# Graph attention: the probability transposes of three units in four moved from TensorE to VectorE blocks and transfers within SBUF

## The chip, the cores and the metric

The kernel runs on one core of one Trainium2 chip. The time is device microseconds for one execution: 1087.12 us, the median of 3 runs (1085.82 to 1088.69).

## The reference

The reference is a small network over 1024 nodes with 512 features and 16384 edges: a graph attention, a linear-attention mixer and a feed-forward layer, and then, on the normalised state `xn`, a second block. This case concerns the graph part of the second block. It has two layers, each of which is a masked attention with 8 heads of 64 features, a projection, a batch norm and a small feed-forward with another batch norm:

```
for l in range(2):                         # two layers
    q, k, v = x @ Wq[l].T + bq[l], x @ Wk[l].T, x @ Wv[l].T      # 1024 x 512 each, 8 heads of 64
    for h in range(8):
        s = q_h @ k_h.T / 8 + log(edge count)                    # 1024 x 1024; no edge: out
        p = softmax(s, axis=-1)
        o_h = p @ v_h                                            # contracts over the 1024 keys
    x = batchnorm(x + o @ Wo[l].T + bo[l]); x = batchnorm(x + ffn(x))
```

The block sums up the code; the rest of the reference (first block, mixers, the final small networks) is not touched.

## The kernel before, in words

The attention of one layer is cut into 64 units (`UNITS`). Unit n is one head with 128 query rows: units 16p to 16p+15 are the two heads of pair p, interleaved, for the eight blocks of 128 rows (`unit`, line 53). A unit's life is this:

1. TensorE makes the scores of two units together (`both_heads`, lines 2079 to 2095) into two PSUM slots of 128 x 1024. There are four slots, given out in the order of the job list (`job_table`), so a job can begin only when the job four places before it has been evacuated (`begin`).
2. VectorE evacuates the scores, takes the mask in and the row extreme with it (line 1522), into one of four buffers `SMs` (`SMB` = 4). It waits before that until the probabilities of unit n-4 have been read.
3. ScalarE takes the exponential in place, with the row sums as by-product (`exp_unit`, line 965).
4. "turn": TensorE transposes the 128 x 1024 probabilities in eight 128 x 128 pieces (line 2137 to 2141, helper line 1793) into a PSUM slot, since the next product contracts over the keys.
5. VectorE (even units) or ScalarE (odd units) copies the slot to SBUF, to `PTr` (`turned`, lines 490 to 499; the copies have lines 1121 and 745). `PTr` has two buffers, one for each group of four units (g % 2).
6. "agg": for each group of four units TensorE multiplies the transposed probabilities with the values (`aggregate`, lines 2070 to 2077), 32 matmuls.

The order in which these steps stand on every engine is written out by hand in `attention_order` (lines 58 to 81): the turn of unit m = n - 4 (`LAG`) stands just before the scores of unit n; between them stand the projections "q" (8 a layer) and "k" (8 a layer), and the steps "rsum" and "rsum_bc" that bring the row sums to the output. PE, VectorE and ScalarE all walk this one list in order, so an instruction that waits holds up all that is behind it on its engine. The queue of SyncE (SP) carries loads of weights in this phase and nothing else (lines 557 to 563); in the first layer it starts with a move of the state within SBUF (line 556).

Of the kernel before, what the change touches and what calls it, by code (L numbers as in the profile page):

```python
# [23 lines left out]
N = 1024  # L24
D = 512
E = 16384
P = 128
# [28 lines left out]


def attention_order():

    order = [("q", 0), ("q", 1), ("k", 0), ("k", 1)]  # L60
    for n in range(0, UNITS + LAG + 4, 2):
        m = n - LAG
        if 0 <= m < UNITS:
            order += [("turn", m), ("turn", m + 1)]
        if n < UNITS:
            order += [("score", n), ("score", n + 1)]
        if m >= 16 and m % 16 == 2:
            order.append(("rsum_bc", m // 16 - 1))
        if n % 8 == 2 and 8 <= n < UNITS - 8:
            order.append(("q", n // 8 + 1))  # L70
        if n == 4:
            order.append(("k", 2))
        if n % 16 == 6 and n < UNITS - 16:
            order.append(("k", 2 * (n // 16) + 3))
        if n % 16 == 14 and n < UNITS - 32:
            order.append(("k", 2 * (n // 16) + 4))
# [33 lines left out]
def job_table():  # L110
# [93 lines left out]
def build(nc, a, out):  # L204
# [5 lines left out]
    with ctx:  # L210
# [48 lines left out]
        bns = sb("bns", [P, 8])  # L259

        psum = ctx.enter_context(nc.psum_tensor("slots", [P, 4, N], fp32))

# [90 lines left out]
        for l in range(L):  # L353
# [60 lines left out]
        agg_rounded, agg_rest, last_agg_rounded, last_agg_rest = (  # L414
            sem(n) for n in ("agg_rounded", "agg_rest", "last_agg_rounded", "last_agg_rest"))
        neg_dst_made, distances_made, dst_rows_ready = sem("neg_dst_made"), sem("distances_made"), sem("dst_rows_ready")
        wqn_loaded, wkn_loaded, bias_rows_loaded, wcol_made, ucol_made = (
# [71 lines left out]

        def turned(eng, copy_out, l, n):  # L490
# [7 lines left out]
            copy_out(PTr[:, g % 2, n % 2, :, n // 2 % 2 * P:(n // 2 % 2 + 1) * P], f"turn{l}g", n,  # L498
                     lambda s: s.rearrange("p (s n) -> p s n", s=TT))

# [12 lines left out]
        def _(sp):  # L513
# [42 lines left out]
            sp.dma_start(SXR[:].bitcast(fp32), XTR[:].bitcast(fp32)).then_inc(state_moved, 16)  # L556
            load_weight("w120")
            load_weight("go0")
            sp.wait_ge(psum_full, INDEX[("agg0g", UNITS // 4 - 1)] + 1)
            sp.dma_start(gv1_whole, a["gv1"].rearrange("(k p) n -> p k n", p=P)).then_inc(gv1_loaded, 16)  # L560
            for name in ("gq1", "gk1", "w121", "go1"):
                load_weight(name)

# [177 lines left out]
        def _(act):  # L741
# [205 lines left out]
            for l in range(L):  # L947
# [24 lines left out]

                pt_free = (psum_full, INDEX[("mixout1", 3) if l == 0 else ("agg0g", UNITS // 4 - 1)] + 1)
                taken = [0]
                for step, n in attention_order():
# [6 lines left out]
                    elif step == "k":  # L982
                        pair, hs = n // 2, slice(n % 2 * D, (n % 2 + 1) * D)
                        if pair >= 2:
                            act.wait_ge(psum_full, INDEX[(f"score{l}g", 16 * pair - 17)] + 1)
                        elif pair == 1:
                            act.wait_ge(*pt_free)
                        src = full(act, f"k{l}g", n)
                        nc.scalar.activation(KS[pair % 2][:, 0, hs], src[:, 0:D], ACT.Copy).then_inc(k_rounded, 1)
                    elif step == "score" and n >= 1:  # L990
                        exp_until(n - 1)
                        if n == 55:
                            round_weight(6 + 3 * l)
                    elif step == "turn":
                        exp_until(n)
                        if n % 2 == 1:
# [70 lines left out]
        def _(dve):  # L1067
# [421 lines left out]
            for l in range(L):  # L1489
# [8 lines left out]
                for step, n in attention_order():  # L1498
# [15 lines left out]
                    elif step == "score":  # L1514
                        src = full(dve, f"score{l}g", n)
                        if n >= SMB:
# [8 lines left out]
                    elif step == "turn":  # L1525
                        if n % 2 == 0:
                            turned(dve, copy_out, l, n)
                    elif step == "rsum":
                        src = full(dve, f"rsum{l}g", n)
# [8 lines left out]
                    elif step == "rsum_bc":  # L1538
# [6 lines left out]
                    if step == "turn" and n % 16 == 15:  # L1545
                        dve.wait_ge(probs, UNITS * l + n + 1)
# [158 lines left out]
        def _(pe):  # L1705
# [364 lines left out]
            def aggregate(slot, l, g):  # L2070

                for s in range(TT):
                    for e in range(2):
                        head = 2 * (g // 4) + e
                        last = mm(slot[e * DH:(e + 1) * DH, 0:2 * P], GV[:, s, head * DH:(head + 1) * DH],
                                  PTr[:, g % 2, e, s, :], s == 0, s == TT - 1)
                return last
# [46 lines left out]
            for l in range(L):  # L2124
                if l:
                    pe.wait_ge(gv1_loaded, 16)
                    token_major(f"gv{l}", gv1_whole, XT, ready=lambda k: state(2 * l, k))
                for step, n in attention_order():
                    slot = begin(f"{step}{l}g", n)
                    if step == "q":  # L2130
# [139 lines left out]
```

## Time and profile before

The profile is of one execution that took 1087.95 us in all; its span, from the first instruction to the last, is 1086.0 us, and 1.95 us lie around it.

| | value |
|---|---|
| median of the runs shown | 1087.12 us |
| the profiled execution, its span | 1087.95 us, 1086.0 us |
| PE busy | 1011.1 us, 93% |
| VectorE busy | 632.7 us, 58% |
| ScalarE busy | 493.8 us, 45% |
| GpSimd busy | 246.3 us, 23% |
| data moved by DMA | 37.43 MB in 18528 packets |

How to read it: PE is TensorE's matmul row, PEld its weight loads, DVE VectorE, ACT ScalarE, POOL GpSimd, SP SyncE; SPq is SyncE's issuing of transfers. "L1522" is line 1522 of the kernel. In the timeline each row has the start and the length in us, the engine, line and operation, what is written and read, the shapes, the count, and in square brackets the idle time before it with what ended it. The attention phases of the two layers stand in the span from about 461 to 679 us and from 769 to 986 us.

### The profile page before, as it was taken

The numbers are of one execution on the slowest core, as the hardware profiler recorded it, in microseconds if no ns is written. First come the engines' busy times: TensorE is split into PE (matmuls) and PEld (weight loads), VectorE is DVE, ScalarE is ACT, GpSimd is POOL, SyncE is SP. The second block draws the span as 40 slices with busy tenths as digits, with TensorE's granted clock in tenths as the row PEclk, the third lists the DMA queues.
The fourth block names the chain that finished last, engine by engine and source line by source line (L and its number), as shares of the span: only waits on it lengthen the run. The fifth ranks groups of instructions, "written<-read, shape, count | busy, mean of one in ns | idle before, by whom it ended". The sixth has DMA issues, their size and how long they took to land.

```text
span 1086.0 us, 15726 instructions
## 1 busy us (share of the span) xinstructions
PE 1011.1 (93%) x5787; PEld 721.4 (66%) x5794; DVE 632.7 (58%) x1087; ACT 493.8 (45%) x766; POOL 246.3 (23%) x137
## 2 busy tenths in 40 slices
PE   6999999999989999999999999989899999999925
PEld 2836556888777868777777776734777777767413
DVE  4785576468693245265656663643556566654495
ACT  1674434555524124065555663122555555651144
POOL 2000000899630513200000073011000000470400
PEclk9999999999999999999999999999999999999977
DMA  9101100002000311400001010210000001100202
GB/s 330 49 0 39 40 9 12 1 1 78 1 1 1 116 39 40 155 1 2 1 1 40 1 40 1 77 39 0 1 2 1 1 1 40 40 1 20 80 1 77
DMA packets 18528, 37.43 MB, mean 34 GB/s; under 512 B 3804, under 2 KB 5020, under 8 KB 17950
## 3 DMA queue, kind: packets, MB, share of 16 engines
q1 hardware_dynamic: 15134, 34.37, 9.2%
q10 hardware_dynamic: 3328, 2.15, 0.6%
q8 instruction: 45, 0.74, 0.3%
q14 instruction: 21, 0.17, 0.1%
HBM read 30.22 MB, written 4.19 MB: 32 GB/s over the span
## 4 chain that ended last, share of the span: by engine, by line
PE 75%; DVE 8%; POOL 7%; issue 6%; ACT 3%; DMA 1%; DVEq 0%; SPq 0%; ACTq 0%; POOLq 0%
PE slots L1726 62%; PE slots L1793 12%; POOL MASK L646 2%; POOL MASK L640 1%; POOL KR L645 1%; DMA W<-in_wkT 1%; POOL X L677 1%; POOL PT L637 1%; DVE XT L1464 1%; DVE PT L1522 1%; ACT X L1050 1%; DVE Q1L L1452 0%; DVE X L1610 0%; DVE XT L1485 0%; POOL WL L657 0%
## 5 line engine op out<-in xcount | busy, mean ns | idle before, releaser
L1121 DVE COPY PT<-slots 128x1024 f32<-128x1024 f32 (+1 forms) x65 | 78.9, 1214 | 71.5 <-PE slots L1793 70.4
L1726 PE MATMUL slots<-PT,XN 128*64 128x256 f32 x1024 | 117.6, 382 | 0.0
L1726 PE MATMUL slots<-KS,QS 64*128 64x512 f32 x768 | 105.6, 406 | 7.5 <-DVE KS L1512 3.1
L701 POOL TENSOR_TENSOR QS<-QF,QS 128x512 fp32r<-128x512 f32 x16 | 20.7, 1291 | 357.0 <-PE slots L1793 327.5
L745 ACT ACTIVATE PT<-slots 128x1024 f32<-128x1024 f32 x68 | 69.7, 1024 | 67.3 <-PE slots L1793 62.4
L1726 PEld LDWEIGHTS slots<-PT,XN 128*64 128x64 f32 x1024 | 70.6, 137 | 42.0 <-issue 8.9
L1522 DVE CUSTOM_DVE_ANT_0 PT<-slots,MASK 128x1024 f32<-128x1024 f32 x64 | 75.8, 1222 | 31.7 <-PE slots L1726 31.7
L1522 DVE CUSTOM_DVE_ANT_0 SM<-slots,MASK 128x1024 f32<-128x1024 f32 x64 | 75.8, 1222 | 29.8 <-PE slots L1726 29.8
L1726 PEld LDWEIGHTS slots<-KS,QS 64*128 64x128 f32 x768 | 69.7, 184 | 28.1 <-issue 6.7
L965 ACT ACTIVATE SM<-SM,nm 128x1024 f32<-128x1024 f32 x64 | 73.2, 1144 | 25.2 <-DVE nm L1522 25.2
L965 ACT ACTIVATE PT<-PT,nm 128x1024 f32<-128x1024 f32 x64 | 73.3, 1146 | 19.4 <-DVE nm L1522 19.4
L1726 PE MATMUL slots<-PT 128*128 128x512 bf16 (+3 forms) x401 | 78.8, 367 | 2.8 <-ACT PT L745 1.2
L1793 PE MATMUL slots<-ident,SM 128*128 128x128 f32 x600 | 73.6, 274 | 2.9 <-ACT SM L965 2.6
L1793 PEld LDWEIGHTS slots<-ident,SM 128*128 128x128 f32 x600 | 67.2, 140 | 11.5 <-DVE nm L1522 4.0
L1793 PE MATMUL slots<-ident,PT 128*128 128x128 f32 x580 | 71.7, 276 | 1.7 <-ACT PT L965 1.4
L1793 PEld LDWEIGHTS slots<-ident,PT 128*128 128x128 f32 x580 | 63.2, 140 | 15.0 <-issue 13.4
L1726 PEld LDWEIGHTS slots<-PT 128*128 128x128 bf16 (+2 forms) x408 | 36.7, 114 | 48.2 <-DVE PT L1283 20.8
L1283 DVE TENSOR_SCALAR PT<-PT 128x1024 bf16<-128x1024 f16 x148 | 64.0, 479 | 0.5 <-PE slots L1726 0.4
L637 POOL TENSOR_SCALAR PT<-PT 128x1024 f32<-128x1024 bf16 x8 | 8.4, 1048 | 186.1 <-ACT PT L861 185.5
L1464 DVE SCALAR_TENSOR_TENSOR XT<-slots,cols,XT 128x1024 f32<-128x1024 f32 x16 | 20.5, 1282 | 36.6 <-PE slots L1726 36.6
L1726 PE MATMUL slots<-SXR,WL 128*128 128x512 f32 x104 | 40.8, 393 | 0.0
L1281 DVE TENSOR_SCALAR PT<-PT 128x128 bf16<-128x128 f16 x61 | 15.2, 249 | 43.6 <-PE slots L1726 43.2
(394 smaller groups left out, 2101.9 us busy)
## 6 DMA issues: line engine op xcount, KB each, us to landing
X<-in_x SPq DMA_DIRECT2D x4, 512.0 KB, 11.5
W<-in_wout SPq DMA_DIRECT2D x2, 1024.0 KB, 6.3
W<-in_gq SPq DMA_DIRECT2D x2, 1024.0 KB, 5.1
W<-in_gk SPq DMA_DIRECT2D x2, 1024.0 KB, 5.2
spill<-X SPq DMA_DIRECT2D x4, 512.0 KB, 2.6
SXR<-XTR SPq DMA_DIRECT2D x1, 2048.0 KB, 8.4
W<-in_w SPq DMA_DIRECT2D x2, 1024.0 KB, 4.9
W<-in_go SPq DMA_DIRECT2D x2, 1024.0 KB, 5.3
```

What stands on the lines that cost most here:

```text
L637: nc.gpsimd.tensor_scalar(negm[:, i % 2, :], adj0[:, i, :], -NEG, NEG, ALU.mult, ALU.add).then_inc(negm_made, 1)
L646: link(nc.gpsimd.tensor_scalar(MASK[:, i, :], MASK[:, i, :], 0.5, NO_EDGE, ALU.is_lt, ALU.mult))
L701: nc.gpsimd.tensor_tensor(QS[:, j % 2, 1, :], QF[:], QS[:, j % 2, 0, :].bitcast(fp32), ALU.subtract).then_inc(q_split, 1)
L745: nc.scalar.activation(dst, src, ACT.Copy).then_inc(act_evacuated, 1)
L965: nc.scalar.activation(SMs[n % SMB], SMs[n % SMB], ACT.Exp, bias=nm[:, n % 8:n % 8 + 1], scale=-1.0, accum_out=ls[:, pair % 2, 2 * t + e:2 ...
L1121: nc.vector.tensor_copy(dst, src).then_inc(dve_evacuated, 1)
L1281: nc.vector.tensor_scalar(dstrow[:, b, :], iota[:, t * P:(t + 1) * P], dst_f[:, bass.ds(g + b, 1)], None, ALU.is_equal)
L1283: nc.vector.tensor_scalar(srcrow[:, b, :], iota, src_f[:, bass.ds(g + b, 1)], None, ALU.is_equal).then_inc(onehot_ready, 1)
L1464: nc.vector.scalar_tensor_tensor(XT[:, c, :], src, col(bias, c), XT[:, c, :], ALU.add, ALU.add).then_inc(dve_evacuated, 1)
L1522: nc.vector.tensor_tensor_reduce(out=SMs[n % SMB], in0=src, in1=MASK[:, unit(n)[2], :], scale=-1.0, scalar=-0.1 * NO_EDGE, op0=ALU.add, op ...
L1726: return nc.tensor.matmul(o_, lhsT, rhs, start=start, stop=stop)
L1793: return nc.tensor.transpose(slot_part, src, ident[0:rows, 0:rows])
```

## The change

What it does:

- A new step "flip" takes the place of "turn" for every unit n below 56 with n % 4 != 0: 42 units a layer, 84 in all. The other 22 units a layer keep their turn. Copies of the turns with n below 56 are all ScalarE's now.
- In a flip VectorE transposes the 32 x 32 blocks of the 128 x 1024 probabilities, SBUF to SBUF, into one of three buffers `FL` of 128 x 1024. The blocks are then in place within themselves, but not on the right partitions.
- SP moves the blocks to `PTr` with 16 transfers a unit, each from 32 partitions to 32 partitions with one contiguous run of 1 KB on each (`move_blocks`). For this `PTr` has another order within a partition (block of 32 queries, then key block, then query). SP waits before a unit's transfers until the flip is done and the `PTr` buffer is free; VectorE waits before a flip until the transfers of three flips before have landed; the aggregation waits until the transfers of its units have landed.
- VectorE's evacuation of scores into an `SMs` buffer waits on the flip of unit n-4, where it waited on the transpose on PE.
- The order list: aggregations stand two units later, and "q", "k" and "rsum_bc" have other places. On SP the loads of `w12` and `go` stand behind the transfers of units 45 and 49; the rounding of `go` on ScalarE goes from unit 55 to 59.
- The program is built with `dynamic_dma_scratch_size=4096`, where it had the default; `FL` needs 12 KB on each partition.

```diff
+FLIPS = [n for n in range(UNITS - 8) if n % 4 != 0]
+FLIP_BUFFERS = 3
+FLIPS_BEFORE = {n: i for i, n in enumerate(FLIPS)}
...
-            order += [("turn", m), ("turn", m + 1)]
+            order += [("flip" if i in FLIPS_BEFORE else "turn", i) for i in (m, m + 1)]
...
-        if m >= 4 and m % 4 == 0:
+        if m >= 6 and m % 4 == 2 and m < UNITS - 4:
+            order.append(("agg", m // 4 - 1))
+        if m in (UNITS - 4, UNITS):
             order.append(("agg", m // 4 - 1))
...
-            engine = {"q": V, "k": V, "score": V, "turn": (V, A)[i % 2], "rsum": V, "rsum_bc": V, "agg": A}[step]
+            engine = {"q": V, "k": V, "score": V, "turn": A if i < UNITS - 8 else (V, A)[i % 2], "rsum": V, "rsum_bc": V, "agg": A}[step]
...
-        PTr = PT[:, 0:8192].rearrange("p (b e s n) -> p b e s n", b=2, e=2, s=TT)
+        PTr = PT[:, 0:8192].rearrange("p (b e u s q) -> p b e u s q", b=2, e=2, u=8, s=TT)
...
+            def move_blocks(l, n):
+                i = len(FLIPS) * l + FLIPS_BEFORE[n]
+                sp.wait_ge(flipped, i + 1)
+                pt_free(sp, l, n)
+                own = FL[:, i % FLIP_BUFFERS, :].rearrange("p (j s q) -> p j s q", s=TT, j=4)
+                for b in range(4):
+                    for j in range(4):
+                        sp.dma_start(PTr[32 * j:32 * j + 32, n // 4 % 2, n % 2, n // 2 % 2 * 4 + b, :, :],
+                                     own[32 * b:32 * b + 32, j, :, :]).then_inc(blocks_moved[i % FLIP_BUFFERS], 16)
...
+                for n in FLIPS:
+                    move_blocks(l, n)
+                    if n == 45:
+                        load_weight(f"w12{l}")
+                    if n == 49:
+                        load_weight(f"go{l}")
...
+                    elif step == "flip":
+                        i = len(FLIPS) * l + FLIPS_BEFORE[n]
+                        dve.wait_ge(probs, UNITS * l + n + 1)
+                        if i >= FLIP_BUFFERS:
+                            dve.wait_ge(blocks_moved[i % FLIP_BUFFERS], 16 * 16 * (i // FLIP_BUFFERS))
+                        nc.vector.transpose(FL[:, i % FLIP_BUFFERS, :].rearrange("p (j s q) -> p s j q", s=TT, j=4),
+                                            SMs[n % SMB].rearrange("p (s j q) -> p s j q", s=TT, j=4)).then_inc(flipped, 1)
...
-                        need(f"turn{l}g", 4 * n + 2, 4 * n + 3)
+                        for i in range(4 * n, 4 * n + 4):
+                            if i in FLIPS_BEFORE:
+                                moved(wait, l, i)
+                            else:
+                                need(f"turn{l}g", i)
```

## Rows read from the trace of the kernel before

**Rows 1.** The page: busy time by engine, and the chain by engine.
```profile
PE 1011.1 (93%) x5787; PEld 721.4 (66%) x5794; DVE 632.7 (58%) x1087; ACT 493.8 (45%) x766; POOL 246.3 (23%) x137
PE 75%; DVE 8%; POOL 7%; issue 6%; ACT 3%; DMA 1%; DVEq 0%; SPq 0%; ACTq 0%; POOLq 0%
```

**Rows 2.** Stretches: length; busy of PE, PEld, DVE, ACT, POOL; clock; DMA share; GB/s.
```profile
468.80:653.10 184.30, 182.11 (x1379) 137.90 (x1376) 114.51 (x168) 109.75 (x168) 29.10 (x14) 1.00 0.04 13
776.90:961.20 184.30, 182.11 (x1379) 138.04 (x1375) 114.55 (x168) 109.77 (x168) 29.02 (x14) 1.00 0.04 13
563.30:576.90 13.60, 13.60 (x103) 10.13 (x101) 8.39 (x14) 8.01 (x13) 1.29 (x1) 1.00 0.00 0
```

**Rows 3.** The chain of waits in order of time: start, us, what (one group of four).
```profile
566.99 1.90 PE slots L1793 x16
568.89 4.56 PE slots L1726 x24
573.45 1.75 PE slots L1793 x16
575.20 1.58 PE slots L1726 x12
576.78 0.21 PE slots L1793
576.99 3.60 PE slots L1726 x32
```

**Rows 4.** Groups of DVE, 563.3 to 576.9 us: count | busy, mean ns | idle before.
```profile
L1522 DVE CUSTOM_DVE_ANT_0 SM<-slots,MASK 128x1024 f32<-128x1024 f32 x3 | 3.6, 1223 | 1.9 <-PE slots L1726 1.9
L1121 DVE COPY PT<-slots 128x1024 f32<-128x1024 f32 x2 | 2.5, 1225 | 2.4 <-PE slots L1793 2.3
```

**Rows 5.** Line 1485, the same size from SBUF to SBUF on DVE: ns min/median/max.
```profile
L1485 DVE TENSOR_SCALAR XT<-XT,bns x10: 804/812/817, 697.1 to 1039.7; 128x1024 f32<-128x1024 f32 x10
```

**Rows 6.** Timeline of SP, transfers issued: start, length (of all xN together).
```profile
356.41 0.37 SPq L528 DMA_DIRECT2D W<-in_q  x1
452.79 0.52 SPq L556 DMA_DIRECT2D SXR<-XTR  x1
986.91 0.82 SPq L517 DMA_DIRECT2D BC<-in_rows  x2
1004.83 0.33 SPq L568 DMA_DIRECT2D X<-spill  x1
1005.84 0.26 SPq L574 DMA_DIRECT2D QZ<-in_nb  x1
1006.14 0.55 SPq L572 DMA_DIRECT2D QZ<-in_nw  x2
1008.84 2.32 SPq L580 DMA_DIRECT2D QZ<-in_nw  x6
1011.20 0.39 SPq L582 DMA_DIRECT2D QZ<-in_nb  x1
```

**Rows 7.** Transfers by line: count, KB each, median us from issue to landing.
```profile
spill<-X SPq DMA_DIRECT2D x4, 512.0 KB, 2.6
SXR<-XTR SPq DMA_DIRECT2D x1, 2048.0 KB, 8.4
```

**Rows 8.** Timeline of DVE and ACT at the first turns of layer 0.
```profile
465.42 1.15 ACT L965 ACTIVATE SM<-SM,nm 128x1024 f32<-128x1024 f32 x1
467.58 1.22 DVE L1121 COPY PT<-slots 128x1024 f32<-128x1024 f32 x1
```

**Rows 9.** Timeline of PE at the last groups of layer 0, and layer 1.
```profile
653.09 3.67 PE L1726 MATMUL slots<-PT,XN 128*64 128x256 f32 x32
656.70 1.97 PE L1793 MATMUL slots<-ident,PT 128*128 128x128 f32 x16
660.17 1.97 PE L1793 MATMUL slots<-ident,SM 128*128 128x128 f32 x16
```

**Rows 10.** Stretches as in rows 2, where PE has little to do.
```profile
1030.00:1040.00 10.00, 7.25 (x34) 4.09 (x32) 8.39 (x21) 2.78 (x4) 0.00 (x0) 1.00 0.00 1
1066.00:1086.00 20.00, 11.82 (x69) 6.68 (x67) 10.02 (x23) 6.57 (x7) 0.00 (x0) 0.84 0.31 105
```

More of the change, by code:

```diff
@@ L63, in attention_order @@
         if 0 <= m < UNITS:
-            order += [("turn", m), ("turn", m + 1)]
+            order += [("flip" if i in FLIPS_BEFORE else "turn", i) for i in (m, m + 1)]
         if n < UNITS:
             order += [("score", n), ("score", n + 1)]
-        if m >= 16 and m % 16 == 2:
+        if m >= 16 and m % 16 == 4 or m == UNITS + 2:
             order.append(("rsum_bc", m // 16 - 1))
-        if n % 8 == 2 and 8 <= n < UNITS - 8:
+        if n % 8 == 4 and 8 <= n < UNITS - 8:
             order.append(("q", n // 8 + 1))
@@ L72, in attention_order @@
             order.append(("k", 2))
[L73 to L76, printed above, removed]
+        if n == 8:
+            order.append(("k", 3))
+        if n % 8 == 0 and 16 <= n < UNITS - 16:
+            order.append(("k", n // 8 + 2))
         if m >= 16 and m % 16 == 0:
             order.append(("rsum", m // 16 - 1))
-        if m >= 4 and m % 4 == 0:
+        if m >= 6 and m % 4 == 2 and m < UNITS - 4:
+            order.append(("agg", m // 4 - 1))
+        if m in (UNITS - 4, UNITS):
             order.append(("agg", m // 4 - 1))
@@ L150, in job_table @@
         for step, i in attention_order():
-            engine = {"q": V, "k": V, "score": V, "turn": (V, A)[i % 2], "rsum": V, "rsum_bc": V, "agg": A}[step]
+            if step == "flip":
+                continue
+            engine = {"q": V, "k": V, "score": V, "turn": A if i < UNITS - 8 else (V, A)[i % 2], "rsum": V, "rsum_bc": V, "agg": A}[step]
             jobs.append(((f"{step}{l}g", i), engine))
@@ L259, in build @@
         bns = sb("bns", [P, 8])
+        FL = sb("FL", [P, FLIP_BUFFERS, N])
         psum = ctx.enter_context(nc.psum_tensor("slots", [P, 4, N], fp32))
@@ L415, in build @@
             sem(n) for n in ("agg_rounded", "agg_rest", "last_agg_rounded", "last_agg_rest"))
+        flipped, blocks_moved = sem("flipped"), [sem(f"blocks_moved{r}") for r in range(FLIP_BUFFERS)]
         neg_dst_made, distances_made, dst_rows_ready = sem("neg_dst_made"), sem("distances_made"), sem("dst_rows_ready")
@@ L488, in row_ready, with pt_free @@
             eng.wait_ge(row_loaded[n % 2], 16 * (n // 2 + 1))
-        def turned(eng, copy_out, l, n):
+        def pt_free(eng, l, n):
             g = n // 4
@@ L497, in turned, with moved @@
                 eng.wait_ge(psum_full, INDEX[("mixout1", 3) if l == 0 else ("gv1", 3)] + 1)
-            copy_out(PTr[:, g % 2, n % 2, :, n // 2 % 2 * P:(n // 2 % 2 + 1) * P], f"turn{l}g", n,
-                     lambda s: s.rearrange("p (s n) -> p s n", s=TT))
+        def moved(wait, l, n):
+            i = len(FLIPS) * l + FLIPS_BEFORE[n]
+            wait(blocks_moved[i % FLIP_BUFFERS], 16 * 16 * (i // FLIP_BUFFERS + 1))
+        def turned(eng, copy_out, l, n):
+            g = n // 4
+            pt_free(eng, l, n)
+            half = n // 2 % 2 * 4
+            copy_out(PTr[:, g % 2, n % 2, half:half + 4, :, :].rearrange("p b s q -> p s b q"), f"turn{l}g", n,
+                     lambda s: s.rearrange("p (s b q) -> p s b q", s=TT, b=4))
         LAST_USE = {
@@ L556, in _ @@
             sp.dma_start(SXR[:].bitcast(fp32), XTR[:].bitcast(fp32)).then_inc(state_moved, 16)
[L557 to L562, printed above, removed]
+            def move_blocks(l, n):
[7 more added lines that the diff above has]
+                                     own[32 * b:32 * b + 32, j, :, :]).then_inc(blocks_moved[i % FLIP_BUFFERS], 16)
+            for l in range(L):
+                if l:
+                    sp.wait_ge(psum_full, INDEX[("agg0g", UNITS // 4 - 1)] + 1)
+                    sp.dma_start(gv1_whole, a["gv1"].rearrange("(k p) n -> p k n", p=P)).then_inc(gv1_loaded, 16)
+                    for name in ("gq1", "gk1"):
+                        load_weight(name)
+                for n in FLIPS:
[4 more added lines that the diff above has]
+                        load_weight(f"go{l}")
             sp.wait_ge(psum_full, INDEX[(f"rsum_bc{L - 1}g", H // 2 - 1)] + 1)
@@ L971, in exp_until @@
                         taken[0] += 1
-                pt_free = (psum_full, INDEX[("mixout1", 3) if l == 0 else ("agg0g", UNITS // 4 - 1)] + 1)
+                second_keys_free = (psum_full, INDEX[("mixout1", 3) if l == 0 else ("agg0g", UNITS // 4 - 1)] + 1)
                 taken = [0]
@@ L986, in _ @@
                         elif pair == 1:
-                            act.wait_ge(*pt_free)
+                            act.wait_ge(*second_keys_free)
                         src = full(act, f"k{l}g", n)
@@ L991, in _ @@
                         exp_until(n - 1)
-                        if n == 55:
+                        if n == 59:
                             round_weight(6 + 3 * l)
@@ L1515, in _ @@
                         src = full(dve, f"score{l}g", n)
-                        if n >= SMB:
+                        if n >= SMB and n - SMB in FLIPS_BEFORE:
+                            dve.wait_ge(flipped, len(FLIPS) * l + FLIPS_BEFORE[n - SMB] + 1)
+                        elif n >= SMB:
                             dve.wait_ge(psum_full, INDEX[(f"turn{l}g", n - SMB)] + 1)
@@ L1544, in _ @@
                             nc.vector.tensor_tensor(AGL[:, n, :], AG[:, n, :], AGR[:, n, :].bitcast(fp32), ALU.subtract).then_inc(last_agg_rest, 1)
-                    if step == "turn" and n % 16 == 15:
+                    if step in ("turn", "flip") and n % 16 == 15:
                         dve.wait_ge(probs, UNITS * l + n + 1)
@@ L2075, in aggregate @@
                         last = mm(slot[e * DH:(e + 1) * DH, 0:2 * P], GV[:, s, head * DH:(head + 1) * DH],
-                                  PTr[:, g % 2, e, s, :], s == 0, s == TT - 1)
+                                  PTr[:, g % 2, e, :, s, :], s == 0, s == TT - 1)
                 return last
@@ L2128, in _ @@
                 for step, n in attention_order():
+                    if step == "flip":
+                        continue
                     slot = begin(f"{step}{l}g", n)
```

7 lines of the change are left out of this document (4 added, 3 removed).

## The prediction

> **What bounds the kernel now.** I read the page first, then stretches of the attention phase, then the chain in order of time, then SP's own timeline. On the page the reader is to see PE busy for 93% of the span and 75% of the chain [rows 1]. In the attention phase it is sharper: from 468.8 to 653.1 us PE is busy for 182.1 of 184.3 us at full clock, DVE for 114.5, ACT for 109.8, and the same in layer 1 [rows 2]. So PE's order of work is the time there. One group of four units takes 13.60 us (the aggregation of one group to that of the next), and on the chain it is made of an aggregation of 3.60, two pairs of transposes of 1.90 and 1.75, and scores and projections between them [rows 3]. DVE and ACT have 5.2 and 5.6 us of slack in those 13.6 [rows 2]. SP has nearly nothing to do there.
>
> **What the change removes.** Four turns cost PE 1.90 + 1.75 = 3.65 us a group on the chain [rows 3], one of them 0.91. Three in four go for the 14 groups below unit 56: 42 x 0.91 = 38.3 us a layer, 76.7 in both. PE's group falls from 13.6 to 10.9 us. Nothing else on PE changes in amount; the new places of "q", "k" and the aggregations move work and cost nothing while PE is not the bound, or a few us at the seams if it is.
>
> **VectorE.** It loses two copies a group (1.22 each) and gains three block transposes of 128 x 1024 in fp32. The trace has no such operation. From both sides: the same size from SBUF to SBUF takes 0.81 us in a scale and shift [rows 5], and 1.22 us from PSUM [rows 4]; twice the latter, 2.4, is my upper end for the strided writing. I take 1.2, the nearest in work per element. DVE's group is 8.39 - 2.44 + 3.66 = 9.6 us, below PE's 10.9 (8.4 and 13.2 at the ends). ScalarE has one copy a group where it had two, so 8.0 falls to 7.0. Neither is the next bound by rows, unless the upper end holds.
>
> **SyncE, the term that decides.** Each flip needs 16 transfers, issued one after the other by one queue: 48 a group, 672 a layer, 1344 in all. The reader is to see in SP's timeline that the issuing itself takes time, whatever the size [rows 6]:
> - One row on one partition, 1.9 KB: 0.26 us, and with its small neighbours a new one every 0.300 us (1005.84 to 1008.84 is ten of them). This is the least that I find.
> - Columns over 40 to 120 partitions, 4 bytes on each, six in a row: 1008.84 to 1011.20, 0.393 us each. These carry next to no data, so it is the issuing that costs.
> - Over 128 partitions: 0.33 alone; two in a row 0.41 each.
> - The one transfer from SBUF to SBUF: 0.52 alone, 0.56 with the 0.04 that lies between two (0.26 against the 0.30 from start to start).
>
> A transfer of the change spans 32 partitions, in a run of 16. I take the 0.393 of the six in a row, nearest in partitions and in being issued without a pause; 0.300 and 0.56 are the ends. So a flip costs SP 16 x 0.393 = 6.29 us and a group 18.9 us, against 10.9 on PE and 13.6 before. SP becomes the bound.
>
> Data is not: 2 MB within SBUF landed in 8.4 us and 512 KB in 2.6 [rows 7], so a unit's 512 KB needs 2 to 3 us of the 6.3. The Trainium skill (DMA: Bandwidth & Descriptors, Issuing engines are not separate DMA queues) says that the time to initiate a transfer "is usually small relative to the DMA itself". For the 512 KB spill the row agrees, 0.33 against 2.6; for these transfers of 32 KB the rows speak against it, since the same 0.3 to 0.5 is paid for a sixteenth of the bytes. By that rule data alone would set the pace and the sum would be that of rival 1.
>
> **How the stall runs.** With three buffers a flip waits until the transfers of three flips before have landed. The next two units' transfers take SP 12.6 us, so DVE has time to fill the free buffer before SP runs dry, and SP stays in work without a gap. DVE, though, stands before each flip; behind it wait the evacuations of scores n+4 and n+5, behind them ScalarE's exponentials, and PE finds no free slot. All of them run at SP's pace. The wait for a free `PTr` buffer isn't late: the aggregation two groups before needs transfers that are three flips older. The weight loads on SP add two issues.
>
> **The sum, by layer.** SP starts when the first flip is done. Its probabilities are ready at 466.6 (465.42 + 1.15) and DVE comes to it at 467.58, so with 1.2 us at 468.8 [rows 8]. It issues 42 x 6.29 = 264.2 us. The last lands some 2.0 us later (2.6 less 0.33 for the spill, and smaller). Then group 13 is aggregated, which before began at 653.09 [rows 9]. What is behind it has got shorter: the turns of 58 and 59 and the scores of 62 and 63 (656.70 to 660.17, 3.5 us) stand before it now and are done meanwhile. The difference is 468.8 + 264.2 + 2.0 - 653.1 - 3.5 = +78.4 us. Layer 1 has the same stretches [rows 2]: +156.8 in both. In general it is 42 x 16 x t - 185.8 for an issue time t, which is nothing at t = 0.276. The profiled execution would go from 1087.95 to 1244.8; the median of the runs shown is 0.8 less: **1244 us**. With 0.300: 1119. With 0.56: 1468.
>
> **Rivals.**
> 1. *The issuing is cheaper than any row* (t below 0.276), since both sides are in SBUF and each row is 1 KB in one piece. Then PE is the bound again at 10.9 us a group and the time is 1087.1 - 76.7 = 1010, with 5 to 15 us back where DVE's 9.6 us come late at the seams: 1010 to 1025; with t between 0.22 and 0.276 it lies between that and 1087. For it: the only transfers in a row with rows of many bytes are loads that compete for memory, and the trace has none of this shape. Against: nineteen small issues in a row and none under 0.25, and the one of this kind is the dearest of those issued alone. It ends on the other side of mine; it decides from 0.276 us down.
> 2. *SBUF to SBUF costs what its one row says*, 0.56: a flip takes 9.0 us, a group 27, and the time is 1468.
> 3. *PE's clock falls too.* In my case PE is busy for 10.9 of 18.9 us, 58%. At 72% busy the granted clock stayed at 1.00, at 59% it was 0.84 [rows 10]. At 1.2 GHz throughout, PE's group would double to 21.8 us and pass SP's 18.9: 28 x (21.8 - 13.6) = +230, some 1317. A part of the time at that level would stay hidden behind SP.
> 4. *The transpose on DVE is slow*, 2.4 us: DVE's group is 13.2, hidden behind SP in my case; without SP's limit it leaves 28 x 0.4 = 11 us of gain, 1076.
>
> **How the numbers follow.** SP bound with t from 0.300 to 0.48: 0.60, by itself 1119 to 1360. SP dearer, or with the clock on top (rivals 2 and 3): 0.17. Rivals 1 and 4, faster: 0.19. Near the balance, within 0.3%: 0.04. A measurement of this kernel can tell about 0.3% from no change. I leave out the lower half of the faster cases and the upper half of the dear ones: 1060 to 1400. Faster 0.19, same 0.04, slower 0.77.
>
> **What would show it.** SP's issues of the new line back to back, 0.3 to 0.5 us from start to start, with hardly a pause between units; a group in about 19 us; DVE's idle time before the flips ended by a DMA; PE busy well under 80% between 469 and the end of the phase, and idle for DVE's evacuations; 1344 more issues and 43000 more packets of 1 KB. The prediction fails if SP idles for the flips (then PE or DVE is the bound and rival 1 holds), if the issues take under 0.276 us, or if the landing takes far over 3 us, in which case the three buffers would be the limit and not the issuing.

## The result, and the profile after

The changed kernel takes **1585.45 us** (median of 4 runs, 1583.95 to 1589.10) where the kernel before takes 1086.47 us: a ratio of 1.459 (95% interval 1.456 to 1.463). The prediction was 1244, with a range of 1060 to 1400. Slower was forecast and is right. The size is missed by 341 us and lies outside the range.

The profile is of the execution of 1589.1 us, whose span is 1587.3 us. First the rows of the page that answer to [rows 1] and [rows 7]: busy time by engine, the chain by engine and by line, and the transfers by line.

```profile
PE 1014.6 (64%) x5122; PEld 696.4 (44%) x5122; DVE 661.7 (42%) x1115; ACT 464.3 (29%) x738; POOL 245.4 (15%) x137
PEclk9999999999996766766765699977677676656996
...
SPq 46%; PE 33%; issue 8%; POOL 5%; DVE 5%; ACT 2%; DMA 2%; DVEq 0%; ACTq 0%; POOLq 0%
...
PT<-FL SPq DMA_DIRECT2D x1344, 32.0 KB, 1.8
```

PE has 665 instructions fewer and is still busy for as long, since its granted clock is at 0.6 to 0.7 of full in the slices of the attention phases. It is no longer the bound: the chain, 75% PE before, is 46% SP's issuing. The kernel has 64500 packets more than before (83047 against 18528); 43008 of them are the blocks' 1 KB rows that the prediction counted, the rest are packets of 4 bytes, 16 a transfer. To see what SP does, look at its timeline within a stretch of the attention phase, and at the new line's own durations (nanoseconds, min/median/max).

```profile
559.68 40.50 SPq L588 DMA_DIRECT2D PT<-FL  x62
```

```profile
L588 SPq DMA_DIRECT2D PT<-FL x1344: 507/591/1843, 470.4 to 1462.4; - x192
...
  DVE FL L1575: 555.6, 78
  PE slots L1775: 450.4, 28
DMA to landing us min/median/max: 1.8/1.8/4.9
```

One row of 62 issues with no pause. Each takes 0.591 us, and the next starts 0.04 us after its end. Two others wait for these transfers: VectorE before 78 of its flips, and PE before every aggregation that uses them (28). SP itself waited for a flip only at the start of the two layers, which its list of waits shows (total, times, longest, in us):

```profile
SPq L588 <- DVE FL L1575: 35.4, 2, 19.9
```

Stretches answer to [rows 2]: 400 us of the attention of layer 0, and one group of four, from one aggregation to the next.

```profile
500.00:900.00 400.00, 173.45 (x1003) 118.88 (x1003) 122.12 (x172) 89.66 (x144) 34.90 (x17) 0.70 0.23 56
564.80:595.40 30.60, 13.59 (x77) 9.22 (x77) 9.67 (x17) 6.78 (x11) 1.27 (x1) 0.72 0.22 52
```

The group takes 30.6 us where it took 13.6 (the others of the layer take 30.4 to 31.9). In it PE works 13.59 us, partly at the lower clock, VectorE 9.67 (the prediction had 9.6), and the DMA engines are busy for 22% of the time. Nothing but SP's instruction stream is full. The rows of PE's timeline that answer to [rows 9] are an aggregation in mid-phase and that of group 13, which closes layer 0's flips; in brackets is the idle time before, and what ended it.

```profile
564.83 6.24 PE L1775 MATMUL slots<-PT,XN 128*64 128x256 f32 x32 [16.16 <-DMA PT<-FL]
```

```profile
906.75 5.95 PE L1775 MATMUL slots<-PT,XN 128*64 128x256 f32 x32 [17.03 <-DMA PT<-FL]
```

Before, the aggregation of group 13 began at 653.09 us and took 3.67; now it begins 253.7 us later. In layer 1 the delay of the same aggregation is 503.1 us, so the second layer adds 249.4.

### The profile page after: what moved, and what is told of

Same layout as the page of the kernel before. It is cut to its first block, busy times and chain, and to the rows that moved or that the text cites. A ratio compares the mean times of both kernels' runs of the same rounds, so it can differ in the third digit from the quotient of the medians.

```text
span 1587.3 us, 15786 instructions
## 1 busy us (share of the span) xinstructions
PE 1014.6 (64%) x5122; PEld 696.4 (44%) x5122; DVE 661.7 (42%) x1115; ACT 464.3 (29%) x738; POOL 245.4 (15%) x137
## 2 busy tenths in 40 slices
DMA packets 83047, 81.57 MB, mean 51 GB/s; under 512 B 25308, under 2 KB 69532, under 8 KB 82462
## 4 chain that ended last, share of the span: by engine, by line
SPq 46%; PE 33%; issue 8%; POOL 5%; DVE 5%; ACT 2%; DMA 2%; DVEq 0%; ACTq 0%; POOLq 0%
SPq L588 46%; PE slots L1775 30%; PE slots L1842 3%; POOL MASK L686 2%; DMA PT<-FL 1%; POOL MASK L680 1%; POOL KR L685 1%; POOL X L717 1%; DMA W<-in_wkT 1%; POOL PT L677 0%; ACT X L1090 0%; DVE Q1L L1492 0%; DVE X L1659 0%; POOL WL L697 0%; DVE SM L1636 0%
## 5 line engine op out<-in xcount | busy, mean ns | idle before, releaser
L1775 PE MATMUL slots<-PT,XN 128*64 128x256 f32 x1024 | 179.8, 527 | 450.4 <-DMA PT<-FL 450.4
L1775 PEld LDWEIGHTS slots<-PT,XN 128*64 128x64 f32 x1024 | 109.4, 194 | 522.0 <-issue 511.0
L1575 DVE STREAM_TRANSPOSE FL<-PT 128x1024 f32<-128x1024 f32 x56 | 69.5, 1243 | 380.4 <-DMA PT<-FL 380.4
L1575 DVE STREAM_TRANSPOSE FL<-SM 128x1024 f32<-128x1024 f32 x28 | 34.9, 1245 | 175.2 <-DMA PT<-FL 175.2
L1842 PE MATMUL slots<-ident,SM 128*128 128x128 f32 x376 | 49.9, 277 | 2.7 <-ACT SM L1005 2.6
L785 ACT ACTIVATE PT<-slots 128x1024 f32<-128x1024 f32 x40 | 40.9, 1023 | 29.7 <-PE slots L1842 24.8
L1842 PEld LDWEIGHTS slots<-ident,SM 128*128 128x128 f32 x376 | 41.0, 140 | 17.2 <-issue 10.8
L785 ACT ACTIVATE AG<-slots 128x256 f32<-128x256 f32 x32 | 12.3, 384 | 118.9 <-PE slots L1775 118.8
L697 POOL TENSOR_TENSOR WL<-W,W2R 128x2048 fp32r<-128x2048 f32 x4 | 18.3, 4570 | 170.5 <-ACT W2R L800 170.5
L1775 PE MATMUL slots<-WL,XTR 128*128 128x512 f32 x96 | 38.2, 398 | 0.0
L677 POOL TENSOR_SCALAR PT<-PT 128x1024 f32<-128x1024 bf16 x8 | 8.4, 1048 | 187.4 <-ACT PT L901 186.8
```

What stands on the lines that cost most here:

```text
L697: nc.gpsimd.tensor_tensor(REST[name][:], split_source(pool, name), ROUNDED[name][:].bitcast(fp32), ALU.subtract).then_inc(w_split, 1)
L785: nc.scalar.activation(dst, src, ACT.Copy).then_inc(act_evacuated, 1)
L1575: nc.vector.transpose(FL[:, i % FLIP_BUFFERS, :].rearrange("p (j s q) -> p s j q", s=TT, j=4), SMs[n % SMB].rearrange("p (s j q) -> p s j ...
L1775: return nc.tensor.matmul(o_, lhsT, rhs, start=start, stop=stop)
L1842: return nc.tensor.transpose(slot_part, src, ident[0:rows, 0:rows])
```

## Experiments

### What one issue costs

The kernel before, with ten issues of each of nine forms and then six one at a time added on SP, in a stretch in which SP is idle and nothing waits for it. Here `issue(to, frm)` is one transfer, `quad` and `other` are different sets of 32 partitions, `at(i)` is the i-th run of 256 columns (1 KB), and `landed()` waits for all transfers so far.

```diff
+            for i in range(10):
+                issue(FL[quad(i), at(i)], MASK[other(i), 0, 0:256])
+            landed()
+            for i in range(10):
+                issue(FL[quad(i), i * 256:i * 256 + 16], MASK[other(i), 0, 0:16])
+            landed()
...
+            for i in range(10):
+                issue(FL[quad(i), at(i)], a["x"][32 * i:32 * i + 32, 0:256])
+            landed()
...
+            for i in range(6):
+                issue(FL[quad(i), at(i)], MASK[other(i), 0, 0:256])
+                landed()
```

> The kernel before, with SP issuing sets of ten small transfers in the stretch of layer 0's attention where its queue is idle; they move nothing that the kernel uses. From start to start, in us, by set: A 32 rows x 1 KB from SBUF to SBUF, B the same with 64 bytes a row, C 128 rows x 1 KB SBUF to SBUF, D 16 rows, E 8 rows, F 2 rows, G 32 rows x 1 KB SBUF to DRAM, H the same DRAM to SBUF, I 128 rows DRAM to SBUF, J as A with a wait for landing after each. Theory 1 (what costs is that both sides lie in SBUF): A 0.63 and B the same, G and H 0.38 to 0.45, J 0.52 for each issue. Theory 2 (a run of transfers over 16 engines costs that much wherever the sides lie, since the generator of descriptors falls behind): A, G and H all near 0.6, J near 0.35. Theory 3 (the bytes hold the queue up): B far under A. If the cost grows with the engines used, E and F are cheaper than A and D (0.3 to 0.45); if with the rows, C is dearer than A. The kernel's time should stay at 1087 under all three.

The kernel's time stayed where it was, 1087.49 us (one run). Rows of line 564 (count, duration in ns min/median/max, first and last start): 32 rows of 1 KB within SBUF, the same with 64 bytes, 128 rows, eight rows, two rows, then SBUF to DRAM, DRAM to SBUF, and last the first form with a wait for the landing after each.

```profile
L564 SPq DMA_DIRECT2D FL<-MASK x10: 556/590/592, 462.2 to 467.9; - x10
...
L564 SPq DMA_DIRECT2D FL<-MASK x10: 507/591/592, 469.7 to 475.3; - x10
...
L564 SPq DMA_DIRECT2D FL<-MASK x10: 511/601/1494, 477.1 to 482.8; - x10
...
L564 SPq DMA_DIRECT2D FL<-MASK x10: 624/625/701, 493.4 to 499.9; - x10
...
L564 SPq DMA_DIRECT2D FL<-MASK x10: 562/563/582, 501.7 to 507.2; - x10
...
L564 SPq DMA_DIRECT2D probe<-MASK x10: 338/421/1137, 508.8 to 512.9; - x10
...
L564 SPq DMA_DIRECT2D FL<-in_x x10: 319/421/422, 515.5 to 519.5; - x10
...
L564 SPq DMA_DIRECT2D FL<-MASK x6: 507/507/553, 528.6 to 537.7; - x6
```

From start to start that is 0.633 us within SBUF ((467.9 - 462.2)/9) and, with 0.04 between two, 0.463 with one side in DRAM. So two things add up against the 0.393 of the prediction. Having both sides in SBUF costs 0.17 us (0.591 against 0.421). Standing in a run costs 0.08 to 0.10 (0.591 against 0.507 alone; 0.421 against 0.32 and 0.34 for the first of a run). Bytes cost nothing that shows: 64 bytes a row take as long as 1 KB. Rows cost little: with 2, 8, 16, 32 and 128 rows the median lies between 0.563 and 0.625, and not in that order. This is theory 1, with 0.463 just above its 0.38 to 0.45.

### One issue a unit

The 16 transfers of a unit become one of the same 512 KB, 128 rows of 4 KB. It leaves the partitions where they are, so the blocks are not brought to their places.

```diff
-                for b in range(4):
-                    for j in range(4):
-                        sp.dma_start(PTr[32 * j:32 * j + 32, n // 4 % 2, n % 2, n // 2 % 2 * 4 + b, :, :],
-                                     own[32 * b:32 * b + 32, j, :, :]).then_inc(blocks_moved[i % FLIP_BUFFERS], 16)
+                sp.dma_start(PTr[:, n // 4 % 2, n % 2, n // 2 % 2 * 4:n // 2 % 2 * 4 + 4, :, :],
+                             own).then_inc(blocks_moved[i % FLIP_BUFFERS], 16)
```

> A flip's 16 transfers of 32 x 1 KB become one of 128 rows x 4 KB, with the same bytes, waits and buffers; the blocks are not permuted, so this part of the computation is left out. Theory 1 (the issuing on SP is the bound, 10.13 us a unit): SP falls to about 0.4 us a unit, PE is the bound again, 1010 to 1025 us. Rival (the latency of flip, transfer and three buffers, or DVE's added work, costs as much as the issuing hid): over 1060.

1025.98 us (1023.12 to 1027.76), ratio 0.943 (0.941 to 0.946). The same bytes, the same flips, the same waits, 559 us less than the changed kernel. So it is not the bytes, the flips or the new order. The rows are 4 KB here and not 1 KB, so the number of packets falls with the number of issues; the next experiment and the one with two queues keep the 1 KB rows and part the two. The stretch from 480 to 620 us shows PE busy for 98% and at full clock, with 42% of the DMA engines' time used:

```profile
480.00:620.00 140.00, 137.22 (x991) 95.69 (x988) 118.52 (x170) 83.65 (x140) 17.07 (x10) 1.00 0.42 162
```

### Eight issues a unit

Eight transfers of 64 rows of 1 KB, so a unit has as many 1 KB rows as in the changed kernel and half the issues. Here too the blocks do not change partitions.

```diff
+                for j in range(4):
+                    for b in range(2):
+                        sp.dma_start(PTr[64 * b:64 * b + 64, n // 4 % 2, n % 2, n // 2 % 2 * 4 + j, :, :],
+                                     own[64 * b:64 * b + 64, j, :, :]).then_inc(blocks_moved[i % FLIP_BUFFERS], 16)
```

> A flip's 16 transfers become 8 of 64 rows x 1 KB, the same bytes; the blocks are not permuted as needed. Theory 1 (time by the number of issues): 5.1 us a unit, 15.2 a group, 2 x (42 x 5.1 - 186) = +56 us, 1140 us. Rival (time by bytes or by packets, which stay the same): 1585, as the changed kernel. Rival (an issue of 64 rows is dearer than one of 32): between 1140 and 1300.

1167.78 us (one run), 28 above what was expected.

```profile
L588 SPq DMA_DIRECT2D PT<-FL x672: 461/597/2077, 468.5 to 1041.0; - x168
```

The median, 0.597, is that of the 32-row form. The mean of a unit is 5.36 us, 0.67 an issue, because some issues take up to 2.08. Those long ones coincide with loads of instructions (below). The packets of 1 KB are as many as before, and 418 us of the 499 are gone with half the issues, so it is the issues that cost. With 42 x 5.36 the prediction's own formula gives 225.1 - 185.8 = +39.3 a layer, 1166.

### One unit in four, within SBUF

```diff
-FLIPS = [n for n in range(UNITS - 8) if n % 4 != 0]
+FLIPS = [n for n in range(UNITS - 8) if n % 4 == 2]
...
-                    if n == 45:
+                    if n == 46:
...
-                    if n == 49:
+                    if n == 50:
```

> Only units with n % 4 == 2 are flipped: 14 a layer, 28 in all, with the 16 transfers each; all else as in the changed kernel. Theory 1: SP needs 10.1 to 10.4 us a group, PE 13.6 - 0.9 = 12.7, so SP is hidden and the gain of 28 x 0.91 = 25 us shows: 1062 us, plus up to 10 where the transfers' latency (10 us of issuing and 2 of landing) comes late for the aggregation. Rival (the flip's latency holds the aggregation up in every group): 1090 to 1150.

1081.84 us (1081.46 to 1083.02), ratio 0.995 (0.994 to 0.997): a small gain, some fifth of the 25 us expected, and outside both the 1062 to 1072 of the theory and the 1090 to 1150 of the rival. SP needs 10.4 us of a group of 12.5 to 13.5, so its rate is hidden, and PE's busy time falls by 20.8 us (1011.1 to 990.3 on the pages). But PE's pauses of over 0.25 us between 440 and 1000 us grew from 16.2 us in sum to 32.7. The rows of PE's waits (whole run), and SP's and the chain's around 943 us, show two of the places:

```profile
PE slots L1775 <- DMA PT<-FL: 7.5, 6, 2.9
```

```profile
931.78 10.96 SPq L588 DMA_DIRECT2D PT<-FL  x16
942.78 0.58 SPq L551 DMA_DIRECT2D W<-in_go  x1
```

```profile
942.78 5.89 DMA W<-in_go
948.67 0.02 issue
948.69 1.06 ACT W2R L800
```

A weight load stands in SP's queue behind a unit's 16 issues, is issued at 942.78, and ends on the chain. PE was done with the weights that it overwrites at 929.1, so it could have gone 13.7 us earlier. I expected SP's cover to be enough once its rate was below PE's; here a queue that is 80% full is also a late queue. The two places account for about half of the 16.5 us that the pauses grew by. The new order of the list was never run by itself, so its share of the rest is not shown.

### Two issuing queues

Six of each unit's 16 transfers are issued by ScalarE, ahead of its later exponentials.

```diff
+                move_part(sp, l, n, lambda b, j: (4 * b + j) % 8 < 5)
...
+                    elif step == "flip":
+                        exp_until(n)
+                        move_part(act, l, n, lambda b, j: (4 * b + j) % 8 >= 5)
```

> The changed kernel with 6 of a flip's 16 transfers issued by ScalarE's queue, the other 10 by SP. Theory 1 (the rate is that of the issuing sequencer): SP needs 10 x 0.633 + 0.1 = 6.4 us a unit and ScalarE 3 x 6 x 0.633 + 7 = 18.4 us a group, so a group falls from 31 to about 19.5 us and the time to 1260 to 1330. Rival (both queues share one generator of descriptors, or the transfers themselves are the limit): no change, 1585, and ScalarE's issues are longer than 0.6 us.

1278.6 us (one run), inside the 1260 to 1330 of the theory, and 307 less than with one queue.

```profile
L525 SPq DMA_DIRECT2D PT<-FL x840: 507/592/1989, 467.3 to 1152.1; - x168
L525 ACTq DMA_DIRECT2D PT<-FL x504: 513/614/1973, 467.3 to 1139.4; - x168
```

Both queues issue at their own 0.59 to 0.61 us at the same time: each of ScalarE's 504 issues overlaps one of SP's, and SP's take 0.592 us in the median beside one of ScalarE's and 0.591 without. The price belongs to the issuing engine; nothing that both share is full. The Trainium skill (DMA: Bandwidth & Descriptors, Issuing engines are not separate DMA queues) holds the time to initiate a transfer to be "usually small relative to the DMA itself". For these transfers of 32 KB the trace disagrees: one takes 0.591 us to issue and lands 1.8 us after the issue's start, a third of the time, and the transfers overlap while the issues do not.

### By way of DRAM, three units in four

A unit's block buffer is stored in DRAM in one transfer, and comes back in four, one for each target set of 32 partitions (32 x 4 runs of 1 KB). Five issues with one side in DRAM take the place of 16 within SBUF. The loads of a unit stand behind the store of the next flipped unit.

```diff
+                sp.dma_start(a["bounce"][i % ROUND], FL[:, i % FLIP_BUFFERS, :]).then_inc(put_out[i % FLIP_BUFFERS], 16)
...
+                sp.wait_ge(put_out[i % FLIP_BUFFERS], 16 * (i // FLIP_BUFFERS + 1))
...
+                blocks = a["bounce"][i % ROUND].rearrange("(b q) (j m) -> j q b m", b=4, j=4)
+                for j in range(4):
+                    to = PTr[32 * j:32 * j + 32, n // 4 % 2, n % 2, half:half + 4, :, :].rearrange("p b s q -> p b (s q)")
+                    sp.dma_start(to, blocks[j]).then_inc(blocks_moved[i % ROUND], 16)
...
+                for at, n in enumerate(FLIPS):
+                    put(l, n)
+                    if at:
+                        get(l, FLIPS[at - 1])
```

> A flip's blocks go to DRAM in one transfer of 128 rows x 4 KB and come back in 4 transfers of 32 rows x 4 runs of 1 KB, the next unit's store ahead of this unit's loads; five issues where there were 16. Theory 1 (number of issues times the price of one with a side in DRAM, 0.46): 2.5 us of SP a unit, 7.5 a group, under PE's 10.9; the time is near that of the one-issue kernel, 1026 to 1045. Rival (bytes: 1 MB a unit through 16 engines; 8 x 0.16 + 32 x 0.06 to 0.09 us an engine, 9.6 to 12.5 us a group): transfers become the bound or come late, 1050 to 1100.

1085.62 us (10 runs, 1080.47 to 1091.54), ratio 1.000 (0.998 to 1.002). The 500 us are gone, but so is the gain: my 1026 to 1045 is missed and the rival with the bytes is right in its number (whether also in its cause is the last experiment's question). The rows are the stretch from 480 to 640 us, and over the whole run PE's waits for the loads, SP's waits for the store and the transfers by line:

```profile
480.00:640.00 160.00, 134.03 (x931) 95.64 (x929) 115.02 (x164) 82.26 (x135) 16.97 (x10) 0.96 0.87 262
```

```profile
PE slots L1788 <- DMA PT<-bounce: 47.1, 21, 4.1
```

```profile
SPq L593 <- DMA bounce<-FL: 34.8, 40, 4.4
```

```profile
bounce<-FL SPq DMA_DIRECT2D x84, 512.0 KB, 4.2
PT<-bounce SPq DMA_DIRECT2D x336, 128.0 KB, 3.7
```

### By way of DRAM, two units in four

```diff
-FLIPS = [n for n in range(UNITS - 8) if n % 4 != 0]
+FLIPS = [n for n in range(UNITS - 8) if n % 4 in (1, 3)]
```

> As the kernel through DRAM, but with two units in four flipped (n % 4 of 1 and 3). Theory 1: 56 turns less, 51 us, less the 10 to 16 us of gaps on PE that the one-issue and the one-in-four kernel show: 1046 to 1055. If the rival of the kernel with three in four holds there, this one, with 6.4 to 8.3 us of transfers in a group of 11.8, should be the faster of the two.

**1048.3 us** (1042.46 to 1051.40), ratio 0.966 (0.964 to 0.968). It lies within the 1046 to 1055 expected, leaves nothing of the reference out and is the fastest such version. The diff is against the version with three units in four by DRAM. The same rows as above: PE busy for 98% at full clock, the DMA engines for 60%, and 5.8 us of waits where there were 47.1.

```profile
480.00:640.00 160.00, 156.08 (x1173) 113.81 (x1171) 108.39 (x161) 103.58 (x160) 31.33 (x15) 1.00 0.60 182
```

```profile
PE slots L1788 <- DMA PT<-bounce: 5.8, 4, 1.8
```

```profile
bounce<-FL SPq DMA_DIRECT2D x56, 512.0 KB, 3.2
PT<-bounce SPq DMA_DIRECT2D x224, 128.0 KB, 3.4
```

### Two units in four, within SBUF

The same choice of units as in the last, with the changed kernel's 16 transfers.

> The changed kernel with two units in four flipped (n % 4 of 1 and 3) and the 16 transfers within SBUF, the control for the kernel through DRAM with the same units. Theory 1 (issuing at 10.36 us a unit, the mean of the changed kernel with its longer issues): 28 units a layer take 290 us, 2 x (290 - 186) = +208, 1295 us. Rival (what made the kernel through DRAM fast is that fewer units are flipped, not the number of issues): near 1048.

1305.31 us (one run). The theory's 1295 is 10 us short, and the rival's 1048 is far off. With 28 units a layer instead of 42 the time above before falls from 499 to 218 us. So of the 537 us between the changed kernel (1585) and the last version (1048), fewer units give back 280 and the way by DRAM, with five issues, 257. Fewer units alone leave the kernel 218 us slower than before; only the way by DRAM turns it into a gain.

```profile
L588 SPq DMA_DIRECT2D PT<-FL x896: 507/591/2201, 468.9 to 1178.2; - x180
```

### By way of DRAM, five units in eight

```diff
-FLIPS = [n for n in range(UNITS - 8) if n % 4 != 0]
+FLIPS = [n for n in range(UNITS - 8) if n % 8 in (1, 2, 3, 5, 7)]
```

> Through DRAM as before, with five units in eight flipped (n % 8 of 1, 2, 3, 5, 7). PE's group falls to 11.3 us; the transfers' engines, busy 0.6 of the time with two in four and 0.8 to 1.0 with three, would be at 0.75 to 0.8. If only the mean share counts: 1035 to 1045, below the 1048 of two in four. Rival (three flips close together in a group of eight bring the queue of transfers up there, as with three in four): 1050 to 1070.

1077.25 us (5 runs, 1071.44 to 1082.77), ratio 0.992 (0.988 to 0.996). A miss of both numbers. The rival's mechanism is in the trace: over the two layers PE waits 13 times for loads, 35.4 us in all, and each time before the aggregation of a group with three flips, never before one with two. Of the versions by DRAM that were run two in four is the best; fewer than two, or another choice of five in eight, was not run.

```profile
480.00:640.00 160.00, 140.70 (x1006) 101.00 (x1006) 107.67 (x157) 90.90 (x143) 19.32 (x11) 0.97 0.76 226
```

### Three in four by way of DRAM, fewer bytes

Do the bytes hold these versions back, or the length of the chain (flip, store, landing, load, landing)? The same five transfers at the same places as in the three-in-four version by DRAM, with a quarter of the store; the loads all read that quarter, so most blocks are another block's. The packets are as many as there, 640 a unit; 128 of them have 1 KB in place of 4.

```diff
-                sp.dma_start(a["bounce"][i % ROUND], FL[:, i % FLIP_BUFFERS, :]).then_inc(put_out[i % FLIP_BUFFERS], 16)
+                sp.dma_start(a["bounce"][i % ROUND, :, 0:256], FL[:, i % FLIP_BUFFERS, 0:256]).then_inc(put_out[i % FLIP_BUFFERS], 16)
...
-                    sp.dma_start(to, blocks[j]).then_inc(blocks_moved[i % ROUND], 16)
+                    sp.dma_start(to, blocks[0]).then_inc(blocks_moved[i % ROUND], 16)
```

> The kernel that moves three units in four by way of DRAM (1085.62 us), with the same five transfers a unit at the same places, but only the first quarter of each unit's columns is stored (128 KB instead of 512 KB, one run of 1 KB per row), and all four loads read that quarter. So a unit moves 640 KB in place of 1 MB; three quarters of the blocks that are loaded are another block's. Theory that the bytes hold it back (the DMA engines at a mean share of 0.87 of their time in the first kernel): the share falls towards 0.87 x 0.625 = 0.54, below the 0.60 of the kernel with two units in four, the loads land in some 3.4 us or less instead of 3.7, the store in under 3.2 instead of 4.2, the aggregations stop waiting, and the time is that of a kernel with three in four hidden on all sides: 1026 to 1045 us. Rival, that the length of the chain holds it back (a store must land before its four loads are issued, the buffers are few, and SP issues in order): the bytes don't matter, the waits for PT<-bounce stay at some 47 us, and the time stays at 1075 to 1090.

1062.34 us (1060.62 to 1065.25), ratio 0.977 (0.975 to 0.978): between the two theories.

```profile
480.00:640.00 160.00, 142.19 (x992) 102.07 (x992) 116.88 (x167) 86.01 (x141) 23.50 (x12) 0.96 0.64 178
```

```profile
PE slots L1788 <- DMA PT<-bounce: 31.8, 19, 5.1
```

Taking 37.5% of the bytes away is worth 23 us of the 60 between the three-in-four version by DRAM (1085.6) and the one-issue kernel (1026.0), which have the same work on PE. So the bytes are a part, and some 36 us stay with them taken away. Two things are seen in those 36. The DMA engines are at 0.64, near the 0.60 of the two-in-four version, and PE still waits 31.8 us for the loads, where the one-issue kernel has no wait for a transfer of blocks at all. And PE's granted clock is lower: with as many instructions as in the one-issue kernel (first row) it is busy for 10.4 us more (second row), at a mean granted clock of 0.96 from 480 to 640 us against 1.00 there.

```profile
PE 940.9 (92%) x5115; PEld 651.6 (64%) x5122; DVE 658.5 (64%) x1115; ACT 460.6 (45%) x738; POOL 246.1 (24%) x137
PE 951.3 (89%) x5115; PEld 663.7 (62%) x5122; DVE 658.3 (62%) x1115; ACT 464.7 (44%) x738; POOL 246.1 (23%) x137
```

The likeliest cause of the waits is the length of the way: a unit's loads stand behind the next unit's flip and store, and PE's group is shorter with three flips in it. The chains of the pages point there. Here are three in four, three in four with fewer bytes, and two in four: DMA and SP's issuing are 16%, 13% and 4% of the chain.

```profile
PE 56%; DMA 11%; DVE 10%; issue 8%; POOL 7%; SPq 5%; ACT 3%; DVEq 0%; ACTq 0%; POOLq 0%
PE 59%; DVE 9%; DMA 9%; issue 7%; POOL 7%; ACT 4%; SPq 4%; DVEq 0%; ACTq 0%; POOLq 0%
PE 71%; DVE 9%; POOL 7%; issue 6%; ACT 3%; DMA 3%; SPq 1%; DVEq 0%; POOLq 0%; ACTq 0%
```

This is read from waits and chains only. No version with its loads moved was run, and none with fewer packets, so the cause of these waits is not shown.

## Why the prediction was wrong

**Right: PE was the bound, and the turns were worth nearly what was put on them.** With the issues taken away and the flips kept, the kernel takes 1026 us, against 1010 to 1025 worked out for rival 1 from [rows 3]. In the two attention phases PE's busy time falls by 73 us (424.4 to 351.2; 76.7 forecast), and its pauses of over 0.25 us grow from 11.7 to 20.5, most of the added ones until VectorE has evacuated scores. So 61 us of the 76.7 are left, the "5 to 15 us back" at its upper end.

**Right: the block transpose.** Taken as 1.2 us between ends of 0.8 and 2.4; it takes 1.245 in the median of either form, 1.20 at the least:

```profile
L1575 DVE STREAM_TRANSPOSE FL<-PT x56: 1201/1245/1246, 474.3 to 1433.4; 128x1024 f32<-128x1024 f32 x56
L1575 DVE STREAM_TRANSPOSE FL<-SM x28: 1239/1245/1247, 469.2 to 1412.5; 128x1024 f32<-128x1024 f32 x28
```

**Right: SP's issuing becomes the bound,** with back-to-back issues, VectorE's flips held for the buffers (555.6 us, 78 times), and PE starved behind them. The landing, 2.0 taken, is 1.8.

**Wrong: the size of the term 42 x 16 x t.** The failing step is "I take the 0.393 of the six in a row". An issue takes 0.633 us from start to start. A unit is 10.13 us where nothing disturbs it (16 x 0.633), and 10.36 in the mean of all 84 units; 17 of the 1344 issues take over 0.9 us. The rest of the formula holds: 42 x 10.36 - 185.8 = +249.3 a layer, twice is +498.6, and 1087 + 499 = 1586 where 1585.45 was measured. The difference to the 264.2 us a layer of the prediction, 171 twice, is the whole of the miss of 341.

The choice was between rows. [Rows 6] hold one transfer within SBUF, 0.52 alone, and rows of loads from DRAM in a run, 0.393. I took the second, as nearest in number of partitions and in being issued without a pause. I put the first in as the upper end, without a run's surcharge; rival 2 and rival 3 had 0.17 together, and the upper half of that was left out of the range. The probe shows that the number of partitions hardly matters, that the sides do, and that the run comes on top. Both terms stood in the trace before. The kernel has two pairs of loads to 128 partitions; in each the first takes 0.34 us and the second 0.43, which is a surcharge of 0.09:

```profile
L517 SPq DMA_DIRECT2D BC<-in_rows x4: 341/390/434, 160.6 to 987.3; - x4
```

The prediction halved the 0.82 of such a pair to 0.41 each, and so did not see it. With the one row within SBUF that gives 0.52 + 0.09 = 0.61 an issue and 0.65 from start to start, 1087 + 2 x (42 x 16 x 0.65 - 185.8) = 1589, within 0.3% of the result. This was found afterwards, with the result known, and the other rows speak less clearly: twelve of the nineteen small loads in a row take 0.25 to 0.29 with no such surcharge, and the six columns 0.32 to 0.42. Rival 2 had the right mechanism with the 0.56 of a lone one, and got 1468.

**The clock (rival 3)** fell as it said: the trace goes back and forth between 2.4 and 1.2 GHz, 0.70 in the mean over the phase, and the aggregation shown takes 6.24 us instead of 3.67. The price that it put on this, up to 1317, did not come. PE's 13.59 us of a group stay well below SP's 30.6, so it cost nearly nothing; at the end of a layer the aggregation of group 13 takes 5.95 and 5.33 us instead of 3.67, some 2 us each.

**The long issues** were not thought of. The page lists two DMA queues that load instructions, 8 and 14. Each of the 17 overlaps a load on queue 8 and ends 0.27 to 0.39 us after it, and no load on queue 8 in SP's stream is without one; the 19 loads on queue 14 coincide with none. Together the 17 add some 14 us to SP's stream. That the load holds the issue up is a reading of these times; no run tested it. In this row of the chain one stands among its neighbours:

```profile
596.01 0.59 SPq L588
596.64 1.63 SPq L588
598.32 0.59 SPq L588
```

## What to carry to other kernels

Before data is moved in many small transfers, count the issues of one queue per round of the loop and multiply by the price of an issue of the same kind in a run, not alone and not of another pair of memories. That product is a bound like an engine's busy time, and it doesn't shrink with the bytes. Where it is too long, take fewer and larger transfers, by way of DRAM if that lets them be merged (16 issues of 0.59 us became 5 of 0.38 and 0.44 in the median), or split them over queues. Then watch the DMA engines' share and the waits for what is loaded: with three units in four they took back more than the third unit gave.

## What the runs showed of the hardware

- An issue from SP takes 0.591 us (0.633 from start to start) in a run when both sides are in SBUF, 0.507 alone; 0.421 (0.463) with one side in DRAM, either way. With 32 rows it is the same for 64 bytes and 1 KB a row, and from 2 to 128 rows it stays within 0.563 and 0.625.
- The queues of SP and ScalarE issue side by side, each at its full rate (0.592 and 0.614).
- Some issues take up to 2.2 us, beside loads of instructions: 17 of 1344 in the changed kernel, all beside queue 8's, and 17 of 672 with eight a unit. The mean unit of 16 is 2% longer than the typical one (10.36 against 10.13), and the unit of 8 by 5% (5.36 against 5.11), mostly by these.
- With stores and loads of 1 MB a unit and the DMA engines at 0.87 of their time, 262 GB/s, a 512 KB store lands in 4.2 us; at 0.60 it takes 3.2, and the spill, with little beside it, 2.6.
- A block transpose of 128 x 1024 in fp32 on VectorE takes 1.245 us.
